# Token tiles of an adapter kernel take every fourth token instead of 128 neighbours

## What is computed

```python
# adapter with layer norm, then residual
h = relu(x @ W1[lang] + b1[lang])             # 512 x 128
a = x + h @ W2[lang] + b2[lang]               # 512 x 512
x = x + layernorm(a) * gamma[lang] + beta[lang]
# linear layer of the sample's category, then residual
x = x + x @ W[cat] + b[cat]
```

## Time and profile before

| | before |
|---|---|
| median of 3 runs | 605.38 us (605.25 to 606.36) |
| the profiled execution | 605.35 us |
| its span, first to last instruction | 603.5 us |
| TensorE busy | 599.0 us (99%) |
| VectorE, ScalarE, GpSimd busy | 522.3, 522.0 and 559.1 us |
| bytes moved by DMA | 165.18 MB, mean 274 GB/s |

### The profile page before, as it was taken

The page is one execution under the profiler, slowest core; times in us unless marked ns, Lnnn a source line. Parts: engine busy times, 40 slices in busy tenths (PEclk is TensorE's granted clock), DMA queues, the critical chain, the costliest instruction groups (busy, mean ns, idle before and its releaser), DMA issues.

```text
span 603.5 us, 10607 instructions
## 1 busy us (share of the span) xinstructions
PE 599.0 (99%) x2881; PEld 494.4 (82%) x2881; DVE 522.3 (87%) x1151; ACT 522.0 (86%) x770; POOL 559.1 (93%) x263
## 2 busy tenths in 40 slices
PE   9999999999999999999999999999999999999998
PEld 7687788888888888888888888888888888888887
DVE  1899898998999988999988989988989988989673
ACT  5878998889898889988899988898988898988770
POOL 5788999999999999999999999999999999999830
PEclk9999999999999999999999999999999999999999
DMA  9999999998999999999999999999999999996222
GB/s 303 281 293 315 300 280 294 281 273 277 285 303 288 283 300 302 308 263 291 287 286 310 301 263 289 275 288 318 250 301 274 292 289 313 300 271 240 87 89 104
DMA packets 123843, 165.18 MB, mean 274 GB/s; under 512 B 11014, under 2 KB 70672, under 8 KB 119716
## 3 DMA queue, kind: packets, MB, share of 16 engines
q1 hardware_dynamic: 123428, 164.28, 95.9%
q10 hardware_dynamic: 288, 0.52, 0.3%
q0 software_dynamic: 96, 0.05, 0.0%
HBM read 131.12 MB, written 33.55 MB: 273 GB/s over the span
## 4 chain that ended last, share of the span: by engine, by line
PE 97%; DVE 1%; ACT 1%; issue 1%; ACTq 0%; DVEq 0%
PE o_bank L876 19%; PE o_bank L878 19%; PE o_bank L877 19%; PE n_bank L895 9%; PE d_bank L876 7%; PE d_bank L878 7%; PE d_bank L877 7%; PE y_bank L876 2%; PE y_bank L878 2%; PE y_bank L877 2%; PE d_bank L908 2%; PE n_bank L908 1%; PE y_bank L884 0%; ACT x_tok L580 0%; PE n_bank L1009 0%
## 5 line engine op out<-in xcount | busy, mean ns | idle before, releaser
L876 PE MATMUL o_bank<-w_hi,x1T_hi 128*128 128x512 f32 x512 | 205.9, 402 | 0.7 <-DVE x1T_lo L760 0.7
L878 PE MATMUL o_bank<-w_hi,x1T_lo 128*128 128x512 f32 x512 | 200.1, 391 | 0.0
L877 PE MATMUL o_bank<-w_lo,x1T_hi 128*128 128x512 f32 x512 | 199.1, 389 | 0.0
L466 POOL TENSOR_TENSOR w_lo<-w_raw,w_hi 128x1024 fp32r<-128x1024 f32 x62 | 148.7, 2436 | 10.2 <-ACT w_hi L554 10.2
L544 ACT ACTIVATE norm<-y,neg_mean_rstd,rstd 128x512 f32<-128x512 f32 x128 | 153.0, 1269 | 0.8 <-DVE neg_mean_rstd L745 0.8
L461 POOL TENSOR_TENSOR x_tok<-x_tok,b_bc 128x1024 f32<-128x1024 f32 x58 | 140.0, 2452 | 1.0 <-DMA b_bc<-in_L_cond_b 1.0
L428 POOL TENSOR_TENSOR xs_lo<-xT,xs_hi 128x2048 fp32r<-128x2048 f32 x28 | 130.2, 4650 | 0.8 <-ACT xs_hi L596 0.2
L695 DVE STREAM_TRANSPOSE xT<-x_quad 128x512 f32<-128x512 f32 x116 | 122.5, 1096 | 0.0
L580 ACT ACTIVATE x_tok<-y,neg_mean 128x512 f32<-128x512 f32 x128 | 91.5, 716 | 31.9 <-DVE neg_mean L715 31.9
L773 DVE TENSOR_TENSOR out_half<-o_bank,b_bc 128x512 f32<-128x512 f32 x127 | 86.9, 684 | 32.1 <-PE o_bank L878 31.5
L878 PEld LDWEIGHTS o_bank<-w_hi,x1T_lo 128*128 128x128 f32 x512 | 96.1, 188 | 21.2
(11 more groups left out here) (101 smaller groups left out, 832.0 us busy)
## 6 DMA issues: line engine op xcount, KB each, us to landing
w_raw<-in_L_cond_W SPq DMA_DIRECT2D x32, 1024.0 KB, 7.1
out<-out_half SPq DMA_DIRECT2D x63, 512.0 KB, 7.9
x_tok<-in_x SPq DMA_DIRECT2D x30, 1024.0 KB, 8.8
x_quad<-in_x SPq DMA_DIRECT2D x116, 256.0 KB, 8.1
w_raw<-in_L_cond_W SPq DMA_DIRECT2D x64, 256.0 KB, 3.9
b_bc<-in_L_cond_b SPq DMA_DIRECT2D x64, 256.0 KB, 7.2
out_half<-in_x SPq DMA_DIRECT2D x2, 512.0 KB, 8.8
x_tok<-in_x ACTq DMA_DIRECT2D x2, 256.0 KB, 3.3
```

The costliest lines, as they stand in the source:

```text
L466: pool.tensor_tensor(w_lo[q][:, c:c + 2, :], w_raw[q][:, c:c + 2, :], w_hi[q][:, c:c + 2, :].bitcast(F32), ALU.subtract).then_inc(w_lo_don ...
L876: pe.matmul(acc, lhs_hi, rhs_hi, start=first, stop=False)
L877: pe.matmul(acc, lhs_hi, rhs_lo, start=False, stop=False)
L878: return pe.matmul(acc, lhs_lo, rhs_hi, start=False, stop=last)
```

## The change

Three patterns in HBM are changed, and with them which token lies where. Before, token tile t held tokens 128t to 128t+127, token 128t+p in partition p. After, tile t holds tokens 4p+t, so partition p holds the four neighbouring tokens 4p to 4p+3, one in each tile. `load_x` then reads one run of 8 KB for each partition instead of four runs of 2 KB; a store of half of the results writes one run of 4 KB for each partition instead of two of 2 KB. The quarters follow the new order of tokens: each still reads runs of 512 bytes (128 features of a token), 16 in each partition, but partition j takes tokens 128m+4j+t, with t outside and m inside, where it took tokens 32b+j. The buffers in SBUF keep their shapes.

```diff
-    x_rows = x.rearrange("s (t p) h -> s p t h", p=P)
-    x_quads = x.rearrange("s (b j) (q f) -> s q j b f", j=SQ, q=NQ)
-    out_rows = out.rearrange("s (t p) h -> s p t h", p=P)
+    x_rows = x.rearrange("s (p t) h -> s p t h", p=P)
+    x_quads = x.rearrange("s (m j t) (q f) -> s q j t m f", t=NT, j=SQ, q=NQ)
+    out_rows = out.rearrange("s (p t) h -> s p t h", p=P)
...
             def load_x_quads(s, p):
                 for n in range(NQ):
-                    sp.dma_start(x_quad[p][quad(n), :, :],
-                                 x_quads[bass.ds(s, 1), n].rearrange("o j b f -> j (o b) f")
+                    sp.dma_start(x_quad[p][quad(n), :, :].rearrange("j (t m) f -> j t m f", t=NT),
+                                 x_quads[bass.ds(s, 1), n].rearrange("o j t m f -> j (o t) m f")
                                  ).then_inc(xq_in[p], 16)
```

## The result

The changed kernel took 606.43 us in the median of 22 runs (605.86 to 609.29), the kernel before 605.38 (604.99 to 607.72): the ratio (of the means over these runs, not of the medians) is 1.0024, with a 95% interval of 1.0016 to 1.0033. It is slower, by little more than the 0.2% that can be told from no change. The median lies inside the range, but that is due to the width of the range: it lies on the slower side, and neither of the slower rivals names the mechanism that turned out to be at work.

The account below looks back on a forecast made before the run. The prediction took TensorE to bound the kernel, at 18.25 us a step with transfers hidden. Its terms, 0 + 0 + 0 on the profiled 605.35 us, gave 605.3 us, range 603.8 to 606.9.

Parts of the forecast that it names:

- the slower rivals: Quarters lose rate: doubled, 670 us, 6 in 100; quarters late in prologue alone: about 607 us, 4 in 100.
- TensorE sets the pace of the steps; transfers are hidden there: In the steps, TensorE takes 18.25 us each with DMA engines full or almost empty; queue time saved counts 0.
- 104,003 packets as worked out: Whole kernel: larger loads of x and stores cut packets from 123,843 to 104,003, with the same bytes.
- the sum: Whole kernel: 0 + 0 + 0 added to the profiled 605.35 us, larger packets gaining nothing in time.
- The quarters: Loads with 512-byte runs in each step: no change expected from the 256 KB stride, still near 208 GB/s.
- The Trainium skill's rule of power-of-two pitches: Quarters' 256 KB stride: by its mildest figure 5.0 us become 5.2, inside the free 2.5; not used in the sum.
- The sign that TensorE's waits in the prologue would be the same: Changed kernel's profile, prologue: TensorE would show the same waits as before, the longest 1.0 and 0.7 us.
- room for the quarters (2.25 us): Prologue: last quarter lands at 47.1 us, VectorE turns it from 49.35, 2.25 us of room, called the tightest place.
- b2 (2.5 us): Steps: b2 issued behind the quarters lands at 320.4 us, GpSimd reads it at 322.92, 2.5 us of room.
- the store (3.1 us): Steps: the half stored from 305.74 us lands at 312.3 and is overwritten from 315.41, 3.1 us of room.

Follow-up runs that it names:

- the kernel of pairs: The changed kernel, but the first sample comes in two loads of two tiles instead of four of one; 609.20 us (before 605.35), ratio 1.0045.

## Why the prediction was wrong

**TensorE sets the pace of the steps; transfers are hidden there.** Right. 18.25 and 18.22 us a step in both kernels, 104,003 packets as worked out, and no wait of TensorE after 75 us. With the first and last samples in the old order the other 30 have the new one throughout, and the time is that of before: the larger packets are worth nothing in the steps, as the sum said.

**The quarters.** The 256 KB stride cost nothing that can be seen. The slowest 5 us around the quarters read as follows (columns as in the earlier trace rows), first in the kernel before, then in the changed one:

```profile
312.00:317.00 5.00, 5.00 (x26) 4.15 (x25) 4.83 (x9) 4.54 (x6) 5.00 (x4) 1.00 1.20 203
312.40:317.40 5.00, 5.00 (x28) 4.23 (x27) 4.47 (x8) 4.80 (x6) 5.00 (x3) 1.00 1.19 203
```

Both move 203 GB/s (208 in the window of the earlier trace rows), and the four quarters issued from 36 to 39 us in the prologue land after 7.5 us (median) for 8.1 before. The Trainium skill's rule of power-of-two pitches (DMA: Bandwidth & Descriptors, "Latency and other measured facts"), which I weighed for the 256 KB, shows nothing here. The 8 KB of the first loads, below any pitch in its figures, did cost.

**The step that failed** are these two sentences of the prediction: "The prologue's single tiles and the last stores keep their packets, only spread over 8 KB steps. What they could cost or save is at most some tenths of a microsecond, on the path only for the last store." Both halves were wrong. The cost is 0.6 to 0.9 us of landing, and they are on the path: the first transposes wait for the tiles, and the second sample's load behind them had no room at all in the profile of before (11.84 us landed, 11.84 us read). The sign that TensorE's waits in the prologue would be the same failed with it, as two waits for `x_tok` are new. I had worked out room for the quarters (2.25 us), b2 (2.5 us) and the store (3.1 us), and taken the quarters for the tightest place of the prologue, but not the one load that TensorE itself reads first thing. That no wait was listed for it meant zero idle time, not slack.

**The second cost** appears in no part of the prediction: a TensorE that waits early in the prologue sometimes stays at the slow pace for almost 7 us more (up to 13.3 us for 6.5) and ends about 3 us later. The slow pace was seen in the kernel of pairs, whose profile fell on such an execution. That the wait brings it on rests on what added matmuls do to the group of long executions, in that kernel clearly, in the changed kernel with less certainty. The changed kernel's own long executions were not profiled; that they look the same inside is inferred.

The mean of all executions carries both: 607.02 us against 605.55, 1.47 us or 0.24%, the ratio measured. The 16 executions of the first group have a mean of 606.33 us, 0.8 us above that of the kernel before (1.0 us by the medians, 1.1 by the two profiled spans), and six of 22 times some 2.55 us more give the other 0.7.

**Open.** Why runs 8 KB apart load more slowly than runs 4 KB apart: the tiles' landings tell the two apart (one kernel at 4 KB, profiled once), not what in HBM or in the engines does it. A larger load of the same bytes was not shown to be better or worse by itself, since the kernel of pairs also moves TensorE's start. Why the pace stays slow in some executions of one kernel and not in others is open too; so is what sets the moment at which it rises, which differs between profiles even where TensorE has no wait.

## What to carry to other kernels

A pattern that makes the large transfers of the steady state longer can make the small first ones scattered; look at the first loads and last stores apart, since they are the ones with nothing to hide behind. Where an engine shows no wait for a transfer, subtract its landing from the first use before calling it hidden: zero idle time may be zero room. Where the first loads may be late by some tenths, cover TensorE's wait with a few matmuls on zeros, which cost less than a start at the slow pace; and look at the list of single executions, as a second group tells of a mechanism that the median hides. Don't read a difference of some tenths of a microsecond between two single profiles as an effect before a repeat shows how much they scatter.

## What the runs showed of the hardware

Four loads of 256 KB in runs of 2 KB, the first of the program, land after 3.2 to 3.3 us (the two from ScalarE's queue, median) when their runs are adjacent or 4 KB apart, and after 3.9 to 4.1 us when they are 8 KB apart. Stores of 128 KB in runs of 1 KB land after 1.7 us with runs 2 KB apart and 1.9 us with 8 KB.

TensorE's pace near the start has two levels, 0.43 and 0.23 us for a pair of 128 by 128 float32 transposes. It rose near 6.5 us in the kernel before, where the engine had worked without a gap since 1.05, and near 13.3 us in the execution that had been idle from 3.98 to 4.84. The moment is not fixed by the work: TensorE did the same from 1.05 us on, without a wait, in five profiles up to the rise, and the pace rose near 4.1 us in one and near 7.1 in another. These are a pair in the first (samples 0 and 31 in the old order) and one in the second (runs 4 KB apart):

```profile
4.18 0.40 PE L1022 MATMUL o_bank<-ident,x_tok 128*128 128x128 f32 x2
...
6.44 0.63 PE L1014 MATMUL n_bank<-ident,x_tok 128*128 128x128 f32 x2
```

This view counts the overlap of a pair in, so that 0.40 us is the fast pace and 0.63 the slow one.

The granted clock reads 1.00, the level of 2.4 GHz, in these stretches as everywhere, so this column did not show it, and the matmuls' own spacing has to be read. Here is that column for one stretch of the slow pace (TensorE busy, granted clock, DMA share, GB/s):

```profile
7.00:8.00 1.00, 1.00 (x7) 1.00 1.05 246
```

A pause does not always bring the slow pace: the changed kernel's profiled execution, whose pace had risen by 4.7 us, was idle for 0.35 us near 5.2 us and went on at 0.24 us a pair; and the kernel with the first sample alone in the new order waited 0.21 us ahead of its first transposes, at the slow pace, and rose near 6.2 us all the same.
